# Query and key products taken load by load of x, and the first gate block's ScalarE queue reordered

## What is computed

```python
qkv = silu(hidden_states @ qkv_w.T)           # 512 -> 3 * 32 * 128
q, k, v = split(qkv)                          # per head
scores = einsum('bhnd,bhmd->bhnm', cq, ck) * diag_decay
attn = scores @ v + carried state             # all heads
gate = sigmoid(hidden_states @ gate_w.T)      # 512 -> 32 * 128
x = layernorm(x + (gate * rmsnorm(attn) * norm_w) @ out_w.T)
x = layernorm(x + ffn(x))                     # base, router, low-rank experts
```

## Time and profile before

| | |
|---|---|
| median of 3 runs | 1025.84 us (1025.33 to 1026.07) |
| profiled execution, its own time | 1024.87 us |
| its span, first to last instruction | 1023.1 us |
| TensorE busy | 1005.1 us (98%), 5620 matmuls |
| weight loads of TensorE | 873.8 us (85%) |
| VectorE / ScalarE / GpSimd busy | 774.2 / 669.1 / 357.9 us (76 / 65 / 35%) |
| mean granted clock in the record | 0.998 |

### The profile page before, as it was taken

One profiled execution on the slowest core, in us unless ns is written; L12 is line 12 of the kernel. 1 busy time (PEld: TensorE's weight loads), 2 busy tenths in 40 slices (PEclk: granted clock), 3 DMA queues, 4 the chain that ended last, 5 costly groups with the idle time before them and its releaser, 6 DMA issues.

```text
span 1023.1 us, 15715 instructions
## 1 busy us (share of the span) xinstructions
PE 1005.1 (98%) x5620; PEld 873.8 (85%) x5620; DVE 774.2 (76%) x1092; ACT 669.1 (65%) x1116; POOL 357.9 (35%) x336
## 2 busy tenths in 40 slices
PE   8999999999999999999999999999999999999996
PEld 6778998889888898889988898888988898888785
DVE  6667976787857977779757878579777797699754
ACT  6567864777557763777647774677637775576635
POOL 1353232342434223433324414432235323322662
PEclk9999999999999999999999999999999999999999
DMA  6021111111211111211111102111111112112302
GB/s 200 26 63 34 65 47 42 55 40 47 68 42 47 47 48 47 62 47 53 47 59 51 47 27 68 42 47 48 59 42 55 52 48 57 32 47 66 112 2 82
DMA packets 48813, 55.44 MB, mean 54 GB/s; under 512 B 4320, under 2 KB 40032, under 8 KB 48736
## 3 DMA queue, kind: packets, MB, share of 16 engines
q1 hardware_dynamic: 48736, 54.44, 17.0%
HBM read 52.33 MB, written 2.10 MB: 53 GB/s over the span
## 4 chain that ended last, share of the span: by engine, by line
PE 87%; DVE 5%; POOL 3%; issue 2%; ACT 2%; DMA 1%; SPq 0%; POOLq 0%; DVEq 0%; ACTq 0%
PE ps L1795 19%; PE ps L1796 19%; PE ps L1797 19%; PE ps L1789 9%; PE ps L1790 8%; PE ps L1791 8%; PE ps L1902 1%; PE ps L1887 1%; DVE wl L1039 1%; PE ps L1904 1%; DVE s L1020 1%; PE ps L1889 1%; POOL rstd L1674 1%; DVE wl L1020 1%; DVE acc L1139 1%
## 5 line engine op out<-in xcount | busy, mean ns | idle before, releaser
L1795 PE MATMUL ps<-xh,wh 128*128 128x512 f32 x658 | 262.0, 398 | 2.8 <-ACT y L490 1.7
L1796 PE MATMUL ps<-xl,wh 128*128 128x512 f32 x658 | 257.2, 391 | 0.0
L1797 PE MATMUL ps<-xh,wl 128*128 128x512 f32 x658 | 256.1, 389 | 0.0
L1695 POOL TENSOR_TENSOR stage<-stage 128x512 f32<-128x512 f32 x61 | 88.0, 1443 | 328.1 <-DMA stage<-stream 328.1
L1715 POOL TENSOR_TENSOR sqacc<-sqacc,sq 128x512 f32<-128x512 f32 x64 | 92.8, 1450 | 276.3 <-ACT sq L537 276.3
L1020 DVE TENSOR_TENSOR wl<-stage,wh 128x1024 fp32r<-128x1024 f32 (+2 forms) x145 | 161.3, 1123 | 34.9 <-ACT wh L378 34.9
L378 ACT ACTIVATE wh<-stage 128x1024 fp32r<-128x1024 f32 (+2 forms) x145 | 122.2, 855 | 54.6 <-PE ps L1791 33.7
L1797 PEld LDWEIGHTS ps<-xh,wl 128*128 128x128 f32 x658 | 123.6, 188 | 26.6
L1795 PEld LDWEIGHTS ps<-xh,wh 128*128 128x128 f32 x658 | 123.5, 188 | 26.7 <-issue 2.1
L1796 PEld LDWEIGHTS ps<-xl,wh 128*128 128x128 f32 x658 | 123.8, 188 | 21.9
L1795 PE MATMUL ps<-wh,xh 128*128 128x256 f32 x392 | 112.8, 288 | 0.0
(11 more groups left out here) (195 smaller groups left out, 2270.0 us busy)
## 6 DMA issues: line engine op xcount, KB each, us to landing
stage<-stream SPq DMA_DIRECT2D x61, 384.0 KB, 3.3
stage<-stream SPq DMA_DIRECT2D x42, 256.0 KB, 2.8
stage<-stream SPq DMA_DIRECT2D x63, 128.0 KB, 2.1
dec<-decay SPq DMA_DIRECT2D x32, 128.0 KB, 2.0
acc<-xt SPq DMA_DIRECT2D x8, 256.0 KB, 5.8
v<-x SPq DMA_DIRECT2D x8, 256.0 KB, 5.4
out<-acc SPq DMA_DIRECT2D x8, 256.0 KB, 2.0
sfull<-lora_router SPq DMA_DIRECT2D x1, 288.0 KB, 5.0
```

What stands on the lines that cost most here:

```text
L1695: nc.gpsimd.tensor_tensor(stage[:, s, 1:5:3, :], stage[:, s, 0:6:5, :], stage[:, s, 7:8, :].broadcast_to([P, 2, U]), ALU.add).then_inc(t_p ...
L1795: nc.tensor.matmul(dst, wt[0], mv_[0], start=start, stop=False, skip_group_check=True)
L1796: nc.tensor.matmul(dst, wt[0], mv_[1], start=False, stop=False, skip_group_check=True)
L1797: return nc.tensor.matmul(dst, wt[1], mv_[0], start=False, stop=stop, skip_group_check=True)
```

## The change

TensorE's q and k phase goes piece by piece of x instead of bank by bank: with one half quarter of x it does all six matmuls, three for each of two banks. The number of matmuls and the sums in the banks stay. In group 0's gate block ACT's queue is put into another order: u2_copy goes ahead of values_hi(0), p5_copy ahead of both qk1 splits, u3_copy ahead of the second, and all three gate outputs ahead of both g23 splits. DVE's two additions go ahead of sums_lo(g23, A). Groups 1 to 7 keep their order.

```diff
@@ -632,6 +632,7 @@
                 scores_hi(0, 1)
                 first_value(7)
                 sums_hi(0, "g01", "B")
+                u2_copy(block_no(0, G01))
                 values_hi(0)
 
             def qk0(g):
@@ -713,6 +714,17 @@
 
             def g01(g):
                 n = block_no(g, G01)
+                if g == 0:
+                    p5_copy(n)
+                    sums_hi(g, "qk1", "A")
+                    u3_copy(n)
+                    sums_hi(g, "qk1", "B")
+                    g11_out(n)
+                    g22_out(n)
+                    g12_out(n)
+                    sums_hi(g, "g23", "A")
+                    sums_hi(g, "g23", "B")
+                    return
                 sums_hi(g, "qk1", "A")
                 u2_copy(n)
                 sums_hi(g, "qk1", "B")
@@ -1299,9 +1311,12 @@
                 n = block_no(g, G01)
                 sums_lo(g, "qk1", "A")
                 sums_lo(g, "qk1", "B")
-                sums_lo(g, "g23", "A")
+                if g > 0:
+                    sums_lo(g, "g23", "A")
                 c22_add(n)
                 c12_add(n)
+                if g == 0:
+                    sums_lo(g, "g23", "A")
                 sums_lo(g, "g23", "B")
 
             def qk1(g):
@@ -1925,26 +1940,33 @@
                                    (wh[:, slot:slot + 2, :], wl[:, slot:slot + 2, :]), hh == 0, hh == HG - 1)
                     last.then_inc(o_done, 1)
 
-            def plain(x_lo_first, hi, lo, unit, bank, start, stop, first=False):
-
-                if first:
+            def first_pieces(piece):
+
+                quarter, k = piece // 2, piece % 2
+                hi, lo = ((xh[:, 0, :], xl[:, 0, :]), (xh[:, 1, :], xl[:, 1, :]),
+                          (x8h, x8l), (xh[:, 3, :], xl[:, 3, :]))[quarter]
+                unit = 2 * (quarter % 2)
+                banks = (B0, B1) if quarter < 2 else (B2, B5)
+                start, stop = piece % 4 == 0, piece % 4 == 3
+                pe.wait_ge(x_hi, piece + 1)
+                if unit + k == 0:
                     pe.wait_ge(t_hi, 1)
-                    for k in range(2):
-                        pe.wait_ge(x_hi, k + 1)
-                        nc.tensor.matmul(ps[:, bank, :], w0h[:, unit, tile(k)], hi[:, half(k)], start=k == 0, stop=False)
+                elif piece == 2:
+                    pe.wait_ge(t_hi, 2)
+                for j in range(2):
+                    nc.tensor.matmul(ps[:, banks[j], :], w0h[:, unit + j, tile(k)], hi[:, half(k)], start=start, stop=False)
+                if piece == 0:
                     pe.wait_ge(t_lo, 1)
-                    for k in range(2):
-                        nc.tensor.matmul(ps[:, bank, :], w0l[:, unit, tile(k)], hi[:, half(k)], start=False, stop=False)
-                    for k in range(2):
-                        pe.wait_ge(x_lo, k + 1)
-                        last = nc.tensor.matmul(ps[:, bank, :], w0h[:, unit, tile(k)], lo[:, half(k)],
-                                                start=False, stop=False)
-                    return last
-                for k in range(2):
-                    pe.wait_ge(x_lo, x_lo_first + k)
-                    last = mm3(ps[:, bank, :], (w0h[:, unit, tile(k)], w0l[:, unit, tile(k)]),
-                               (hi[:, half(k)], lo[:, half(k)]), start and k == 0, stop and k == 1)
-                return last
+                elif piece == 2:
+                    pe.wait_ge(t_lo, 2)
+                for j in range(2):
+                    nc.tensor.matmul(ps[:, banks[j], :], w0l[:, unit + j, tile(k)], hi[:, half(k)], start=False, stop=False)
+                pe.wait_ge(x_lo, piece + 1)
+                for j in range(2):
+                    last = nc.tensor.matmul(ps[:, banks[j], :], w0h[:, unit + j, tile(k)], lo[:, half(k)],
+                                            start=False, stop=stop)
+                    if stop:
+                        last.then_inc(d_done, 1)
 
             def first_value(t):
 
@@ -1964,18 +1986,8 @@
                 last.then_inc(d_done, 1)
 
             def first_group():
-                x1 = (xh[:, 0, :], xl[:, 0, :])
-                x2 = (xh[:, 1, :], xl[:, 1, :])
-                x4 = (xh[:, 3, :], xl[:, 3, :])
-                plain(1, *x1, 0, B0, True, False, first=True)
-                plain(1, *x1, 1, B1, True, False)
-                pe.wait_ge(t_lo, 2)
-                plain(3, *x2, 2, B0, False, True).then_inc(d_done, 1)
-                plain(3, *x2, 3, B1, False, True).then_inc(d_done, 1)
-                plain(5, x8h, x8l, 0, B2, True, False)
-                plain(5, x8h, x8l, 1, B5, True, False)
-                plain(7, *x4, 2, B2, False, True).then_inc(d_done, 1)
-                plain(7, *x4, 3, B5, False, True).then_inc(d_done, 1)
+                for piece in range(8):
+                    first_pieces(piece)
                 for t in range(4):
                     first_value(t)
                 scores(0, 0)
```

## The result

The changed kernel took **1021.37 us** (median of seven runs, 1019.68 to 1021.87); seven runs of the kernel before on the same chip gave 1023.43 (1021.45 to 1026.07). The ratio is 0.9971, with a 95% interval of 0.9958 to 0.9984, which is a gain of about 3.0 us (1.6 to 4.3); the two medians themselves lie 2.06 apart. The profiled execution took 1021.64 with a span of 1019.9, 3.2 less than before. A second comparison of the same two kernels (experiment 5) gave 0.9959 (0.9944 to 0.9974). The two intervals overlap.

The account below looks back on a forecast made before the run. TensorE, busy nearly all the time, was taken as the bound, with gains only where it idles or runs slowly: 1.67 + 1.38 + 2.09 - 0.5 = 4.64 us off the median 1025.84 gives 1021.2, range 1019.3 to 1023.1.

Parts of the forecast that it names:

- Terms 2 and 3: First gate block: bank copy ahead of the values split gains 1.38 us, gate outputs ahead of g23 splits 2.09 us.
- D: Rival, first gate block: POOL's late g23 sum delays a bank copy and the next block's matmuls; 1023.0 us, chance 0.12.
- Term 1: Q and k phase: going by load of x removes TensorE's wait, value matmuls start at 18.72, gain 1.67 us.
- E: Rival, q and k phase: changing bank at every matmul costs 3.8 us in all, leaving 1025.0; chance 0.05.
- If the clock rises after the same length of unbroken work: Q and k phase: assumption under which 48 matmuls from 5.04 end at 18.72, a gain of 1.67 us.
- Other bound: Q and k phase: the clock rises at 7.97 at the earliest, making the gain 2.81 us.
- B: Rival, q and k phase: the clock rises at the old moment, total gain 3.75, 1022.1 us; chance 0.15.
- A new stall of 0.5 us: Second head's scores: the later qk2 load delays POOL's sum and ACT's split past the slack, costing 0.5 us.
- It landed 3.95 us after issue: Load of qk2: the old time from issue to POOL's start, carried over, puts landing at 55.7 us.
- F: Rival, second head's scores: a qk2 load taking 8.6 us or more makes the kernel slower than before; chance 0.03.
- Everything after the first group slides as a block: Later groups: they keep the whole gain, as TensorE waits for little else and loads slide along.

Follow-up runs that it names:

- experiment 8: Changed kernel with the first gate output also ahead of the second qk1 split, so the qk2 load goes out later; 1022.15 us in a single run.
- experiment 1: Kernel before with only TensorE's new q and k order, old ACT and DVE queues; 1021.92 us, ratio 0.9977 to the kernel before.
- experiment 3: Changed kernel with ACT's square and third bank copy ahead of the qk2 split in the first group; 1019.39 us, ratio 0.9949 to the kernel before.
- experiment 2: Changed ACT and DVE queues with TensorE's old q and k order; 1022.71 us, ratio 0.9976 to the kernel before.
- experiment 6: Changed kernel with the values split behind both qk1 splits and two bank copies each one split later; 1020.67 us, ratio 0.9960.
- experiment 9: Version of experiment 7 with POOL's second addition of squares in the first group waiting for k's last splits; 1018.97 us, ratio 0.9950.
- experiment 7: Changed kernel with the edits of experiment 6 and nine instead of six starting matmuls on zeros; 1020.44 us, ratio 0.9954.
- experiment 11: Kernel before with nine instead of six starting matmuls on zeros; 1024.72 us in a single run.

## Why the prediction was right, and where it was not

The sign and the size held: 1021.2 forecast, 1021.37 measured, inside 1019.3 to 1023.1. The closeness of the median is largely luck, for two errors met in it. The gain beside the kernel before was smaller than forecast (3.0 or 4.2 in the two comparisons, against 4.64). And the 1025.84 it was taken off was the median of three runs at the upper end for that kernel; the seven runs beside the changed kernel have 1023.43. Taken off that, the forecast gain gives 1018.8, below the stated range. In the profiled spans, where 4.64 was forecast and 3.2 came, the terms are: the q and k phase 0.42 more than forecast, the gate block as forecast, the stall 1.20 more, and 0.64 lost in the rest, for which nothing was put down.

**Terms 2 and 3** held to the second decimal: 1.38 + 2.09 = 3.47 forecast, 3.46 measured, the same in every run with the gate part but experiment 8, which undid a piece of it. No matmul waited, so D (a late sum of g23) did not come: ACT began g23's splits at 52.42 and copied the bank at 54.21.

**Term 1** had the wait right: it is gone. V was forecast at 18.72 and came at 18.30 and 18.70 in the two runs of this kernel, though the first real matmul of the first, held by x's DMA, was 0.27 later. E is out: two banks in turn keep a pace of 0.227. The rule behind the number did not hold. "If the clock rises after the same length of unbroken work" meant the 5.4 us from 6.94 to 12.3; from the first real matmul to the rise it was 4.0 and 5.4 in the two runs of this kernel, 2.6 in experiment 1 and nothing in experiment 3. That V came near 18.72 in these two runs is luck; in the other four of the new order with six zeros it lies at 16.77 to 18.19.

Also "Other bound: the warmup's 2.93 us of unbroken work brought no rise, so the earliest is 5.04 + 2.93 = 7.97" was wrong. The pace doubled at 7.4 in experiment 1 and before 4.95 in experiment 3. Taking one run's lack of a rise for a bound treated a moment that moves from run to run as a property of the work; the term's range should have gone to about 3.6, the gain in V of experiment 3. The Trainium skill's sentence in the prediction ("TensorE: Matmul & The Clock Gate") that this moment is not tied to the kernel's start agrees with these runs: before 4.95 us to 10.5 us with one and the same order and six zeros.

Over six runs with the new order and six zeros V is 17.8 in the mean, against 20.6 over three with the old, so the term is worth some 2.7 us rather than 1.67 at V. At the end, experiment 1's ratio of 0.9977 is 2.4 us (1.4 to 3.4). B (the old moment, 12.3) was not seen in any run of the new order. The three rises of the old order lie at 12.3 to 12.7 and the six of the new before 10.6, so the order of work moves the moment too; how, these runs don't show.

**"A new stall of 0.5 us"** is the main step that failed, in size and not in kind. It was 1.70 and 1.29 in the two runs of this kernel. The issue came as forecast, 7.17 us after the first gate matmul (forecast 51.7 - 44.55 = 7.15). "It landed 3.95 us after issue" did not carry over: POOL began 54.55 - 49.63 = 4.92 after it. The sum took 3.59 instead of 3.49. That makes 0.02 + 0.97 + 0.10 = 1.09 later, and with the 0.5 a stall of 1.59, against 1.70. The 0.97 lies in SP's second DMA issue, 1.70 us long instead of 0.44; from its end to POOL's start it is 2.85 in the changed kernel, 3.14 in the kernel before. The issue was long in four runs of the new order (1.70, 1.22, 1.86, 1.30 in experiment 3) and short in the others, experiments 2 and 8 among them. It is not the only way to the stall: in experiment 2 it was short, and a sum of 3.96 us in place of 3.49 made most of the difference. Why the issue takes so long there stays open: nothing was tried on it. F (slower) had the right mechanism and, as forecast, far too little delay to turn the sign.

In experiments 6 and 9 the load is early enough and the wait goes; 0.86 and 0.47 of the stall are left. DVE splits that are long beside POOL operations lie there in both. In experiment 9 holding POOL back did shorten k's splits; that the rest of it has the same cause is argued from the rows. The Trainium skill ("SBUF — State Buffer", section "Who interferes with whom") says that these two block each other when DVE reads both inputs from SBUF and GpSimd reads SBUF too; the 0.68 and 0.69 of k's splits with POOL held back, against 1.89 for the pair beside it in experiment 7 and 2.55 in experiment 6, agree.

"Everything after the first group slides as a block" was also too simple. The rest varies by 2.7 us over the thirteen profiles, and took 0.64 in the changed kernel. That this is chance is argued from its spread, not shown by an edit.

## What to carry to other kernels

When an in-order queue is reordered so that a result goes out earlier, follow the step that was pushed back to the last instruction that it frees: here a split 1.0 us later was a load 1.0 us later, and past its slack each further us of it was a us of TensorE. Don't give a moment that moves from run to run a bound from one run, and don't carry a load's landing time to another moment without a range. Once a stall is found, a second may stand right behind it: taking away ACT's wait of 1.75 won 0.84 of 1.70, and holding POOL back for one addition made k's two splits short but the stretch only 0.14 shorter. And don't take a forecast off a median of three runs when later runs of the same kernel may lie 2 us lower.

## What the runs showed of the hardware

- TensorE's pace at the start is 0.43 us a matmul, which is 1.2 GHz, and doubles at a moment that moves from run to run. With six zeros and the new order it came between 4.4 and 4.95 us at the earliest (experiment 3) and at 10.5 at the latest, with the old order at 12.3 to 12.7; with nine zeros it came between 4.2 and 7.5. The record of the granted clock reads full speed throughout.
- In two runs the pace was slow ahead of a pause and full behind it: a pause of 0.59 us before 4.95 in experiment 3, and one of 1.38 us after nine zeros and one real matmul in experiment 11, where the matmuls from 7.79 on go at 0.235.
- DVE's subtraction with two inputs in SBUF took up to 2.6 times its time beside a POOL operation: 1.80 for 0.69, 2.33 and 2.07 for 1.23.
- One DMA issue of SP took 1.22 to 1.86 us in four runs, where the same issue took 0.43 to 0.44 in the others.
